# Decoder block with a routed expert stage: the first pair's work moved in between the last tile's steps, the first list made after twelve tiles

## The chip, the cores and the metric

The kernel runs on one NeuronCore of a Trainium2 chip. The time is the device time of one execution in microseconds (us). Engines in the texts: PE (TensorE, matmuls), DVE (VectorE), ACT (ScalarE), POOL (GpSimd) and SP (SyncE, which only issues transfers here). Each engine takes its instructions strictly in the order in which they are written and waits on semaphores. Transfers are issued by SP, ACT and POOL and run on 16 DMA engines that all three share.

## The reference: what is computed

x is 16 tiles of 128 tokens by 256 numbers. A layer norm and a latent self attention are added to x, then a layer norm and a cross attention with 32 heads, then a layer norm and a mixture of 32 experts:

```python
x = x + _L0_attn_ref(_layernorm(x), ...)
x = x + _L0_xattn_ref(_layernorm(x), ctx_2048, ctx_2048, mask, ...)
x = x + _L0_ffn_ref(_layernorm(x), ...)
# in the last: softmax of x @ gate.T, the top experts until their share reaches 0.8 (at most 8),
# for each of them  h = silu(x @ w_gate.T) * (x @ w_up.T);  out += (h @ w_down.T) * weight
```

Tokens pick their own experts, so which rows an expert handles is known only once tokens are routed. The kernel keeps seven experts of each token, so it has 16 x 128 x 7 = 14336 rows to send through experts.

## The kernel before, in words

**Two stages.** In the tile stage 16 tiles pass through both attentions and the router, two or three at a time in flight. In the pair stage 144 blocks of 128 rows, each of one expert, are handled two at a time: 72 pairs, called pair 0 to 71.

**What sets the order.** The tile stage is written by the table `AT`: for each engine it gives every step a time within a tile, and tile b has it `PERIOD` (18.74) times b later. `ORDER` sorts all of them, and each engine's instructions are emitted in that order. The numbers are only a sort key. Steps in `ONCE` stand once. The pair stage is a plain loop over q on each engine, after the table's steps.

**From tile to rows.** For each tile DVE builds `rowb` (the normalized rows, made in `n3`, and the experts' weights, last written in `g13`), and POOL sends it out seven times by index (`sc0` to `sc6`, line 418) to `rows` in memory, into the regions of seven experts. From tile 13 on POOL clears a small buffer between two of them (`pause`, line 416). After tile 15's seven, POOL's queue goes on with the pairs' results (line 428).

**Lists.** Which block belongs to which expert is worked out from the counts in `stack` and `seen4`. A first list of 52 blocks (`NA`) is made by the steps `la1`, `la2`, `la3` on PE and DVE, from the blocks that the first `SEEN` tiles have filled. SEEN is 14 before. A second list of 92 blocks is made within pairs 2 and 4. The blocks are taken in the order of four groups of tiles (`EPOCH`, by the last tile of each), so that tokens of early tiles are finished early.

**One pair q.** SP loads its two blocks to a slot of four (`xblk`, line 313). PE transposes them (`T_`, line 1261), ACT copies that (`xt`), PE multiplies by the expert's gate and up weights (`gu`, line 1283, four matmuls for a block of the two), ACT takes the tanh (`tanh`, line 570), DVE reads the block's weight and target rows (`meta`, lines 920 to 931) and forms the product (`ab`, lines 936 and 942), PE transposes it (`hT_`), ACT copies (`hts`), PE multiplies by the down weights (`dn`, line 1309), ACT copies (`yc`), POOL scatters two blocks of results to `parts` in memory (line 428). A slot of results and of target rows is used again four pairs later: `meta(q)` ends with a write of `dst[q % 4]` (line 931) that waits until both scatters of pair q-4 have landed.

**Final sums.** `FETCH` says in which pair ACT issues the load of a finished tile's seven partial results (896 KB). Three pairs later DVE does `first_sums` (lines 948 and 950), and four pairs later `other_sums` (957, 959, 961), at the end of its iteration. Tiles 12 to 15 are summed after the last pair. SP stores them.

**PSUM.** Five banks form a ring that the tile stage's steps take in PE's order. A step waits until the use five before it has been read.

## Time and profile before

| | us |
|---|---|
| runs shown (3) | 663.89, 668.93, 669.28 |
| median | 668.93 |
| profiled execution, time | 669.07 |
| profiled execution, span | 667.3 |

| engine | busy us | share of the span |
|---|---|---|
| PE | 564.1 | 85% |
| DVE | 421.5 | 63% |
| POOL | 347.5 | 52% |
| ACT | 345.7 | 52% |

The profiled execution lies 0.14 us above the median, and its own time is 1.77 us longer than its span. The busy share is an average over two stages with other limits: PE is nearly always busy in the tile stage (to about 350 us), less so between the stages, and in the pair stage (from 361 us) it has gaps. A row of the timeline gives the start, the length, the engine, the line and the operation, and in brackets how long the engine had been idle before it and what ended that. Busy time is not a reason in itself: each step of the prediction asks which wait ends last.

### The profile page before, as it was taken

Reading aid. Unit: us, or ns where it says so; the run is one execution under the profiler, and the core shown is the slowest. Engines: PE = TensorE matmul, PEld = TensorE weight load, DVE = VectorE, ACT = ScalarE, POOL = GpSimd, SP = SyncE. Lnnn points to the kernel's source line nnn. Section 1 sums busy time; section 2 is a strip of 40 time slices with the busy share of each in tenths; the row PEclk is TensorE's granted clock in tenths of the full one; section 3 lists DMA queues with packets and bytes.
Section 4 is the critical chain, followed back from the end, with each engine's and each line's share of the span. In section 5 each row is a group of like instructions: output and inputs, shape, how many; then the busy total and the mean of one; then the engine's idle time right before and its main releaser. Section 6 shows DMA issues by size and latency. Waiting matters only on the chain.

```text
span 667.3 us, 13791 instructions
## 1 busy us (share of the span) xinstructions
PE 564.1 (85%) x3365; PEld 432.5 (65%) x3365; DVE 421.5 (63%) x1934; ACT 345.7 (52%) x853; POOL 347.5 (52%) x508
## 2 busy tenths in 40 slices
PE   3699999999999999999775869889988888788860
PEld 1467777767777767776554657767767777677750
DVE  1366777778877777877666435444544456774884
ACT  2366667766666767666541425445444454443530
POOL 3122165556656556565556755554544556554551
PEclk9999999999999999999985979999998899997995
DMA  6401337622221212211114757656534468886855
GB/s 177 163 22 44 119 115 209 165 76 64 76 73 64 73 64 78 67 67 66 67 48 139 224 165 233 200 186 184 158 99 130 134 189 280 277 258 209 254 176 182
DMA packets 50750, 93.00 MB, mean 139 GB/s; under 512 B 9991, under 2 KB 39343, under 8 KB 50483
## 3 DMA queue, kind: packets, MB, share of 16 engines
q1 hardware_dynamic: 34642, 43.74, 23.1%
q0 software_dynamic: 12288, 32.15, 13.3%
q10 hardware_dynamic: 3744, 16.24, 7.5%
q8 instruction: 32, 0.52, 0.3%
q14 instruction: 44, 0.35, 0.2%
HBM read 52.73 MB, written 43.54 MB: 144 GB/s over the span
## 4 chain that ended last, share of the span: by engine, by line
PE 61%; issue 10%; ACT 8%; DVE 6%; SPq 5%; DMA 4%; another core or an unknown queue 4%; POOL 1%; POOLq 0%; ACTq 0%; DVEq 0%
PE bank L1283 11%; PE bank L1309 6%; PE bank L1112 5%; ACT KA L514 4%; PE bank L1136 4%; PE bank L1001 4%; PE bank L1113 4%; PE bank L1143 3%; PE bank L1261 3%; PE bank L1162 3%; PE bank L1081 3%; PE bank L1158 3%; ACT Q L436 2%; PE bank L1299 2%
## 5 line engine op out<-in xcount | busy, mean ns | idle before, releaser
L428 POOL DMA_INDIRECT parts<-PT,dst x108 | 109.2, 1011 | 91.9 <-ACT PT L436 57.3
L418 POOL DMA_INDIRECT rows<-rowb,idx x112 | 111.2, 993 | 58.3 <-DVE rowb L814 31.1
L1283 PE MATMUL bank<-wgu_sb,PT 128*128 x576 | 131.3, 353 | 10.2 <-issue 8.8
L1283 PEld LDWEIGHTS bank<-wgu_sb,PT 128*128 128x128 f32 x576 | 95.1, 199 | 28.4 <-issue 27.5
L436 ACT ACTIVATE PT<-bank 128x512 f32<-128x512 f32 (+1 forms) x158 | 77.5, 514 | 51.2 <-PE bank L1309 20.8
L1309 PE MATMUL bank<-wd_sb,VC 96*128 x288 | 79.1, 398 | 21.6 <-ACT VC L436 13.2
L936 DVE SCALAR_TENSOR_TENSOR PT<-PT,bank 128x192 f32<-128x192 f32 x72 | 25.5, 354 | 111.6 <-ACT PT L570 76.9
L714 DVE TENSOR_REDUCE NM<-bank 128x4 f32<-128x512 f32 x128 | 80.5, 681 | 3.0 <-PE bank L1113 2.7
L436 ACT ACTIVATE VC<-bank 96x256 f32<-96x256 f32 (+1 forms) x104 | 46.5, 447 | 63.7 <-PE bank L1299 23.3
L1309 PEld LDWEIGHTS bank<-wd_sb,VC 96*128 96x128 f32 x288 | 52.3, 195 | 32.6 <-issue 27.8
L530 ACT ACTIVATE PT<-bank,padcol 128x512 f32<-128x512 f32 x96 | 59.7, 693 | 15.0 <-PE bank L1143 15.0
L1112 PE MATMUL bank<-KA,Q 96*128 96x512 f32 x128 | 58.6, 458 | 2.8 <-ACT Q L436 0.7
L428 POOL DMA_INDIRECT parts<-wq_sb,dst x36 | 36.6, 1018 | 35.1 <-ACT wq_sb L436 25.1
L1113 PE MATMUL bank<-maskn,nident 128*128 128x512 f32 x128 | 50.7, 396 | 0.0
L1261 PE MATMUL bank<-con,pool_a 128*128 128x128 f32 x288 | 46.5, 287 | 2.7 <-DMA pool_a<-rows 2.0
L570 ACT ACTIVATE PT<-bank 128x192 f32<-128x192 f32 x72 | 23.8, 331 | 47.8 <-PE bank L1283 27.3
L1261 PEld LDWEIGHTS bank<-con,pool_a 128*128 128x128 f32 x288 | 37.5, 148 | 12.7 <-DMA pool_a<-rows 5.7
L942 DVE SCALAR_TENSOR_TENSOR PT<-PT,wsl,bank 128x96 f32<-128x96 f32 x144 | 38.8, 312 | 2.6
L366 POOL TENSOR_TENSOR scalars<-scalars 128x1 f32<-128x1 f32 x64 | 36.9, 576 | 5.0
L364 POOL TENSOR_TENSOR scalars<-mv_ln,scalars 128x1 f32<-128x1 f32 x48 | 9.7, 203 | 57.1 <-DVE mv_ln L620 56.7
L514 ACT ACTIVATE KA<-bank,con 96x128 fp32r<-96x128 f32 x128 | 34.4, 367 | 9.5 <-PE bank L1100 9.5
L436 ACT ACTIVATE Q<-bank 96x512 fp32r<-96x512 f32 (+1 forms) x48 | 34.9, 728 | 6.5 <-PE bank L1121 3.7
(243 smaller groups left out, 1140.4 us busy)
## 6 DMA issues: line engine op xcount, KB each, us to landing
pool_a<-rows SPq DMA_DIRECT2D x144, 148.5 KB
wgu_sb<-wgu_d SPq DMA_DIRECT2D x8, 768.0 KB
pool_a<-parts ACTq DMA_DIRECT2D x5, 896.0 KB
KA<-parts ACTq DMA_DIRECT2D x5, 896.0 KB
...
```

The costliest lines, as they stand in the source:

```text
L418: gp.indirect_dma_start(out=rows, out_offset=bass.IndirectOffsetOnAxis(ap=idx[b % 2][:, k:k + 1], axis=0), in_=rowb[b % 2][:, :], in_offse ...
L428: gp.indirect_dma_start(out=parts, out_offset=bass.IndirectOffsetOnAxis(ap=dst[q % FEED][:, j:j + 1], axis=0), in_=yb[q % FEED][:, j, :], ...
L436: return ac.activation(o, i, ACT.Copy)
L514: last = ac.activation(KA[b % 2][0:CR, g, :], o[0:CR, hf * P:(hf + 1) * P], ACT.Copy, scale=own8[0:CR, g:g + 1])
L530: ac.activation(PT[:, i, :, :].rearrange("p h n -> p (h n)"), ring_bank(f"s{i}", b)[:, :], ACT.Exp, bias=padcol[:, pad_of:pad_of + 1], sca ...
L714: v.tensor_reduce(NM[:, hg, at:at + HG * HG].rearrange("p (g h) -> p g h", h=HG)[:, :, hg], ring_bank(f"mx{u}", b)[:, :].rearrange("p (g m ...
L942: last = v.scalar_tensor_tensor(hv[q % 2][:, j, :], av[q % 2][:, j, :], wsl[q % 2][:, j:j + 1], halves[:, j, NI:2 * NI], ALU.mult, ALU.mult)
L1112: t.matmul(o[:, :], Q2[b % 2][0:CR, hf, hg, :], KA[b % 2][0:CR, HG * hf:HG * hf + HG, :].rearrange("p g m -> p (g m)"), start=True, stop=F ...
L1113: t.matmul(o[:, :].rearrange("p (g m) -> p g m", g=HG), nident[:, :], maskn[:, b * P:(b + 1) * P].unsqueeze(1).to_broadcast([P, HG, P]), s ...
L1261: last = t.transpose(XT_PS[q % 2][:, j * D + k * P:j * D + (k + 1) * P], xblk[q % FEED][:, j, k * P:(k + 1) * P], ident)
L1283: last = t.matmul(GU_PS[q % 2][:, j * 2 * NI:(j + 1) * 2 * NI], xTb[q % 2][:, j, k * P:(k + 1) * P], wgu_sb[:, k, one_of(expert[i]), :].sq ...
L1309: last = t.matmul(Y_PS[q % 2][:, j * D:(j + 1) * D], hTb[q % 2][:, j, :], wd_sb[:, one_of(expert[2 * q + j]), :].squeeze(1), start=True, s ...
```

## The change

Five edits:

1. `EPOCH` becomes (5, 11, 13, 15) and `SEEN` becomes 12. So `la1`, `la2` and `la3`, whose keys hang on SEEN, come two tiles earlier in PE's and DVE's order, and SP's first loads wait for twelve tiles' rows.
2. Steps `T0`, `T1`, `gu0` (PE), `xt0`, `xt1`, `tanh0` (ACT), `meta0`, `ab0` (DVE) enter the table, at places within tile 15. They are the same instructions that stood behind the table's steps.
3. SP waits for the last use of `x1` only before pair 2. The four slots are handed out in another order, so that pairs 0 and 1 don't lie over `x1`.
4. The matmul that places the padding rows (line 1319 before) and the DVE copy of its result come after pair 0's `dn` and after `ab(1)`.
5. `FETCH` puts tiles 6 to 13 at pairs 60, 61, 62, 65, 66, 67, 70, 71. Before it was 57, 59, 61, 63, 65, 67, 69, 71. In DVE's loop `other_sums` now stands ahead of `first_sums`.

```diff
-EPOCH = (5, 10, 13, 15)
-SEEN = EPOCH[2] + 1
+EPOCH = (5, 11, 13, 15)
+SEEN = EPOCH[1] + 1
...
-FETCH = {**{44 + 2 * b: b for b in range(6)}, **{57 + 2 * b: 6 + b for b in range(5)}, **{67 + 2 * b: 11 + b for b in range(3)}}
+FETCH = {**{44 + 2 * b: b for b in range(6)}, **{q: 6 + n for n, q in enumerate((60, 61, 62, 65, 66, 67, 70, 71))}}
...
+           ... "T0": 45.5 + (NB - 1) * PERIOD, "T1": 46 + (NB - 1) * PERIOD, "gu0": 52 + (NB - 1) * PERIOD ...
+           ... "xt0": 47 + (NB - 1) * PERIOD, "xt1": 49 + (NB - 1) * PERIOD, "tanh0": 53 + (NB - 1) * PERIOD ...
+           ... "meta0": 53 + (NB - 1) * PERIOD, "ab0": 57.4 + (NB - 1) * PERIOD ...
...
-        xblk = [... for n in range(FEED)]
+        xblk = [... for n in (2, 3, 0, 1)]
...
-            sp.wait_ge(S["x1b"], NB)
             sp.wait_ge(S["x1nT"], NB)
             for q in range(NPAIR):
+                if q == 2:
+                    sp.wait_ge(S["x1b"], NB)
...
-            xt(0)
-            xt(1)
-            tanh(0)
...
-            meta(0)
-            dve.wait_ge(S["tab"], 5)
-            v.tensor_copy(tbl_i[:, 2 * NBLK:], HT_PS[1][:, 0:NE]).then_inc(S["lists"], 1)
-            ab(0)
             for q in range(NPAIR):
                 if q + 1 < NPAIR:
                     meta(q + 1)
                 late_read(q)
                 if q + 1 < NPAIR:
                     ab(q + 1)
+                if q == 0:
+                    dve.wait_ge(S["tab"], 5)
+                    v.tensor_copy(tbl_i[:, 2 * NBLK:], HT_PS[1][:, 0:NE]).then_inc(S["lists"], 1)
                 late_list(q)
-                if q - 3 in FETCH:
-                    first_sums(FETCH[q - 3])
                 if q - 4 in FETCH:
                     other_sums(FETCH[q - 4])
                     summed.append(FETCH[q - 4])
+                if q - 3 in FETCH:
+                    first_sums(FETCH[q - 3])
...
+            def gu0(_):
+                pe.wait_ge(S["lists"], 1)
+                pe.wait_ge(S["wgu"], 8 * 16)
+                gu(0, 0)
+                gu(0, 1)
...
-            T_(0)
-            T_(1)
-            gu(0, 0)
-            gu(0, 1)
-            vacated(4)
-            pe.wait_ge(S["pick"], 3)
-            t.matmul(HT_PS[1][:, 0:NE], ones[:, :], pickp[:, :], start=True, stop=True).then_inc(S["tab"], 1)
             for q in range(NPAIR):
...
                 dn(q)
+                if q == 0:
+                    vacated(4)
+                    pe.wait_ge(S["pick"], 3)
+                    t.matmul(HT_PS[1][:, 0:NE], ones[:, :], pickp[:, :], start=True, stop=True).then_inc(S["tab"], 1)
```

The first place is PE's queue at the end of tile 15, from its second transpose of the values (`vt1`) to its product `wo`. Before:

```order
L1172 MATMUL bank3<-con,VC 128x128 x3
L996 MATMUL bank4<-con,pool_a 128x128 [waits s_on,s_eall]
L996 MATMUL bank4<-con,pool_a 128x128
L1226 MATMUL bank5<-pick,ones 128x104 [waits s_pick,s_cums]
L1001 MATMUL bank6<-wo_sb,pool_a 128x256 [waits s_oT2_sb,s_on]
L1001 MATMUL bank6<-wo_sb,pool_a 128x256
L996 MATMUL bank7<-con,rowb_1 128x128 [waits s_x2n,s_pt]
```

Now:

```order
L1169 MATMUL bank4<-con,VC 128x128 x3
L1231 MATMUL bank0<-con,pool_a 128x128 [waits s_bl0]
L1231 MATMUL bank0<-con,pool_a 128x128 x3
L1231 MATMUL bank1<-con,pool_a 128x128 [waits s_bl1]
L1231 MATMUL bank1<-con,pool_a 128x128 x3
L993 MATMUL bank5<-con,pool_a 128x128 [waits s_on,s_xT_sb]
L993 MATMUL bank5<-con,pool_a 128x128
L998 MATMUL bank6<-wo_sb,pool_a 128x256 [waits s_oT2_sb,s_eall]
L998 MATMUL bank6<-wo_sb,pool_a 128x256
L1243 TENSOR_LOAD tbl_i [waits s_wgu,s_lists]
L1253 MATMUL bank2<-wgu_sb,PT 128x192
L993 MATMUL bank7<-con,rowb_1 128x128 [waits s_x2n,s_on]
```

The list's matmul (line 1226) has gone from between `oT` and `wo`, eight transposes of pairs 0 and 1 stand ahead of `oT`, and pair 0's gate and up products (the register load and four such matmuls in all, the first shown) stand between `wo` and `xT`.

The second place is DVE's queue in tile 14's stage, between the last normalization of tile 13's heads (`on`) and the eight maxima of tile 14 (line 714 before, 712 now). Before:

```order
L725 TENSOR_TENSOR pool_a<-bank6,rdx_1 128x128 [waits s_rdx]
L675 TENSOR_REDUCE scalars<-bank1 128x1 [waits s_ss]
L714 TENSOR_REDUCE NM<-bank7 128x4 [waits s_cT,s_mx]
L714 TENSOR_REDUCE NM<-bank3 128x4 [waits s_mx]
L714 TENSOR_REDUCE NM<-bank4 128x4 [waits s_mx]
L714 TENSOR_REDUCE NM<-bank5 128x4 [waits s_mx]
```

Now:

```order
L723 TENSOR_TENSOR pool_a<-bank3,rdx_1 128x128 [waits s_rdx]
L854 COPY scalars<-bank4 128x1 [waits s_tab]
L856 TENSOR_TENSOR scalars<-scalars 128x1 [waits s_cums]
L857 SCALAR_TENSOR_TENSOR scalars<-scalars,cob 128x1
L826 TENSOR_SCALAR ge<-cob,scalars 128x52
L860 SCALAR_TENSOR_TENSOR oh,scalars<-cob,scalars,ge 128x52 [waits s_cums]
L829 TENSOR_SCALAR pick<-oh,cob 128x52 [waits s_cums]
L830 SCALAR_TENSOR_TENSOR pick<-cob,scalars,oh 128x52
L673 TENSOR_REDUCE scalars<-bank1 128x1 [waits s_ss]
L712 TENSOR_REDUCE NM<-bank4 128x4 [waits s_cT,s_mx]
```

The seven instructions of `la2` now stand ahead of tile 14's maxima. The four of `la3` come after the fourth of the eight.

The third place is DVE's queue in the pair stage where tiles 6 and 7 are summed, with the pair's own instructions between them left out here. Before, one half of a tile's sums stood in each iteration:

```order
L957 TENSOR_TENSOR VC<-NM 128x256 [waits s_fsum,s_out2]
L959 TENSOR_TENSOR VC<-VC,pool_a 128x256 [waits s_fsum]
L961 TENSOR_TENSOR VC<-VC,x2 128x256 [waits s_fsum]
L948 TENSOR_TENSOR NM<-KA 128x512 [waits s_fin1]
L950 TENSOR_TENSOR NM<-NM,KA 128x512 [waits s_fsum]
```

Those five are now one iteration's (line numbers two lower), with nothing of a pair between them:

```order
L955 TENSOR_TENSOR VC<-NM 128x256 [waits s_fsum,s_out2]
L957 TENSOR_TENSOR VC<-VC,pool_a 128x256 [waits s_fsum]
L959 TENSOR_TENSOR VC<-VC,x2 128x256 [waits s_fsum]
L946 TENSOR_TENSOR NM<-KA 128x512 [waits s_fin1]
L948 TENSOR_TENSOR NM<-NM,KA 128x512 [waits s_fsum]
```

In the iterations of pairs 64, 65, 69 and 70 DVE has both halves to do, and none in those of 60, 61, 62 and 67.

## Rows read from the trace of the kernel before

**Rows 1.** Windows view, core 0: busy time of each engine, PE's granted clock, DMA share
```profile
348.00:350.00 2.00, 0.75 (x7) 0.55 (x7) 1.83 (x12) 0.00 (x0) 1.50 (x3) 1.00 0.12 41
362.00:364.00 2.00, 2.00 (x9) 1.68 (x8) 1.83 (x14) 1.19 (x2) 1.72 (x3) 0.50 0.76 241
388.00:392.00 4.00, 4.00 (x20) 3.65 (x20) 2.57 (x17) 1.18 (x3) 2.75 (x3) 0.72 0.65 183
...
608.90:647.00 38.10, 33.00 (x183) 26.63 (x182) 31.77 (x152) 18.63 (x42) 21.44 (x21) 1.00 0.71 227
```

**Rows 2.** Timeline, pair stage's start: start us, length us, engine, line, operation, idle before
```profile
361.16 1.94 PE L1261 MATMUL bank<-con,pool_a 128*128 128x128 f32 x8
363.02 2.92 PE L1283 MATMUL bank<-wgu_sb,PT 128*128 x8
363.26 0.15 DVE L876 TENSOR_SCALAR cc<-bank 128x2 f32<-128x2 f32 x1
366.64 0.82 PE L1283 MATMUL bank<-wgu_sb,PT 128*128 x4
```

**Rows 3.** Timeline, POOL's chain up to pair 4
```profile
357.89 1.03 POOL L418 DMA_INDIRECT rows<-rowb,idx  x1 [2.41 <-DVE rowb L814]
...
380.27 1.01 POOL L428 DMA_INDIRECT parts<-PT,dst  x1 [0.30 <-issue]
382.64 1.00 POOL L428 DMA_INDIRECT parts<-PT,dst  x1 [1.36 <-ACT wq_sb L436]
...
385.55 0.16 DVE L931 TENSOR_TENSOR dst<-ksl,pool_a 128x2 int32<-128x2 f32 x1 [5.26 <-DMA parts<-PT,dst]
...
386.61 0.80 PE L1246 MATMUL bank<-pick,ones 128*128 128x184 f32 x2 [3.85 <-issue]
```

**Rows 4.** Timeline, tile 15's last steps
```profile
350.21 0.41 PE L996 MATMUL bank<-con,pool_a 128*128 128x128 f32 x2 [1.37 <-DVE pool_a L725]
350.65 0.38 ACT L436 ACTIVATE pool_a<-bank 128x256 f32<-128x256 f32 x1 [3.40 <-PE bank L996]
352.04 1.31 PE L1001 MATMUL bank<-wo_sb,pool_a 128*128 128x256 f32 x4
356.07 0.66 PE L996 MATMUL bank<-con,rowb 128*128 128x128 f32 x2 [2.73 <-DVE rowb L623]
```

**Rows 5.** Timeline of DVE, the list's steps la2 and la3 in tile 15's stage
```profile
349.97 0.15 DVE L856 COPY scalars<-bank 128x1 f32<-128x1 f32 x1
351.35 0.27 DVE L832 SCALAR_TENSOR_TENSOR pick<-cob,scalars,oh 128x52 f32<-128x52 f32 x1
352.24 0.21 DVE L835 CAST tbl_i<-bank 128x52 int32<-128x52 f32 x1 [0.62 <-PE bank L1226]
352.61 0.26 DVE L838 TENSOR_SCALAR mine<-bank,cob 128x52 f32<-128x52 f32 x1
```

**Rows 6.** Timeline of DVE and PE, tile 14's eight maxima and what follows
```profile
311.65 5.01 DVE L714 TENSOR_REDUCE NM<-bank 128x4 f32<-128x512 f32 x8 [0.70 <-PE bank L1113]
316.81 0.63 PE L1121 MATMUL bank<-con,NM 128*128 128x128 f32 x4
```

**Rows 7.** Chain of waits from 596 us: start us, length us, what
```profile
618.52 0.60 DVE NM L948
...
619.76 0.43 DVE con L920 x4
...
620.52 0.16 DVE dst L931
...
621.56 0.35 DVE VC L957
...
622.73 0.04 DVE con L920
...
627.20 5.73 DMA parts<-PT,dst
...
651.79 2.63 DMA parts<-wq_sb,dst
```

More of the change, by code:

```diff
@@ L61 @@
     "SP": {"ldx": -6.0, "ldc": -2.0, "n3": 42.5, **{f"w{n}": 25.0 + 12.0 * n for n in range(10)}}}
-ONCE = {"mi", "mk", "la1", "la2", "la3"} | {f"w{n}" for n in range(10)}
+ONCE = {"mi", "mk", "la1", "la2", "la3", "T0", "T1", "gu0", "xt0", "xt1", "tanh0", "meta0", "ab0"} | {f"w{n}" for n in range(10)}
 ORDER = {e: [(s, b) for _, s, b in sorted((at + PERIOD * b, s, b) for s, at in steps.items() for b in range(NB) if s not in ONCE or b == 0)] for e, steps in AT.items()}
@@ L554, in g1 @@
                 ac.activation(ev[b % 2][:, 0:NE], ring_bank("lg", b)[:, 0:NE], ACT.Exp, bias=nlmax[b % 2][:, :]).then_inc(S["eall"], 1)
-            schedule("ACT", {"mk": mk, "r3": r3, "r7": r7, "r8": r8, "r10": r10, "r11": r11, "r12": r12, "r15": r15, "r16": r16, "r17": q_rows(0), "r17b": q_rows(1),
-                      "kv": kv, "kT": kT, "c": c, **{f"s{i}": s_(i) for i in range(6)}, "pv0": pv(0), "pv1": pv(1),
-                      "oT": oT_, "xT": xT, "g1": g1})
             def xt(q):
@@ L868, in la3, with meta @@
                 listed(0, NA, ring_bank("la3", 0))
-            schedule("DVE", {"la1": la1, "la2": la2, "la3": la3, "mi": mi, "mk": mk, "r1": r1, "r2": r2, "r4": r4, "r5": r5, "r6": r6, "r7": r7, "r9": r9, "r10": r10, "r13": r13, "r14": r14, "r16": r16,
+            def meta(q):
+                dve.wait_ge(S["bl"][q % FEED], 32 * (q // FEED + 1))
+                if 2 * q == NA:
+                    dve.wait_ge(S["lists"], 5)
+                if q >= 2:
+                    dve.wait_ge(S["bv"], nth("bv", q - 2))
+                for j in range(2):
+                    i = 2 * q + j
+                    last = v.scalar_tensor_tensor(wjnk[:, 2 * (q % 2) + j, :], iota_e, tbl_f[:, i:i + 1], xblk[q % FEED][:, j, D:D + NE], ALU.is_equal, ALU.mult,
+                                                  accum_out=wsl[q % 2][:, j:j + 1])
+                last.then_inc(S["w"], 1)
+                for j in range(2):
+                    i = 2 * q + j
+                    last = v.scalar_tensor_tensor(kjnk[:, 2 * (q % 2) + j, :], xblk[q % FEED][:, j, D + NE:D + NE + TOP], mine[:, i:i + 1], iota_k, ALU.is_equal, ALU.mult,
+                                                  accum_out=ksl[q % 2][:, j:j + 1])
+                last.then_inc(S["k"], 1)
+                dve.wait_ge(S["k"], nth("k", q))
+                if q >= FEED:
+                    stored(dve, q - FEED)
+                v.tensor_tensor(dst[q % FEED][:, :], ksl[q % 2][:, :], xblk[q % FEED][:, :, ROW - 1], ALU.add).then_inc(S["dst"], 1)
@@ new lines, in ab @@
+            def ab(q):
+                halves = GU_PS[q % 2][:, 0:4 * NI].rearrange("p (j n) -> p j n", j=2)
+                dve.wait_ge(S["th"], nth("th", q))
+                v.scalar_tensor_tensor(av[q % 2], th[q % 2], 1.0, halves[:, :, 0:NI], ALU.add, ALU.mult).then_inc(S["av"], 1)
+                dve.wait_ge(S["av"], nth("av", q))
+                dve.wait_ge(S["w"], nth("w", q))
+                if q >= 2:
+                    dve.wait_ge(S["hT"], nth("hT", q - 2))
+                for j in range(2):
+                    last = v.scalar_tensor_tensor(hv[q % 2][:, j, :], av[q % 2][:, j, :], wsl[q % 2][:, j:j + 1], halves[:, j, NI:2 * NI], ALU.mult, ALU.mult)
+                last.then_inc(S["bv"], 1)
@@ L871, in _ @@
+            schedule("DVE", {"meta0": lambda _: meta(0), "ab0": lambda _: ab(0), "la1": la1, "la2": la2, "la3": la3, "mi": mi, "mk": mk, "r1": r1, "r2": r2, "r4": r4, "r5": r5, "r6": r6, "r7": r7, "r9": r9, "r10": r10, "r13": r13, "r14": r14, "r16": r16,
                       "kv": kv, **{f"mx{u}": mx(u) for u in range(8)}, "vt0": on(0), "vt1": on(1), "wo": wo_, "n3": n3,
@@ L1285, in gu, with vacated, late @@
                 last.then_inc(S["gu"], 1)
+            def gu0(_):
[3 more added lines that the diff above has]
+                gu(0, 1)
+            schedule("PE", {"T0": lambda _: T_(0), "T1": lambda _: T_(1), "gu0": gu0, "la1": la1, "la2": la2, "la3": la3, "r3": r3, "r4": r4, "r6": r6, "r7": r7, "r8": r8, "r9": r9, "r11": r11, "r12": r12, "r13": r13, "r15": r15, "r16": r16,
+                      "r17": q_half(0), "r17b": q_half(1), "kv": kv, "kT": kT, **{f"mx{u}": mx(u) for u in range(8)}, "c": c,
+                      **{f"s{i}": s_(i) for i in range(6)}, "pv0": pv(0), "pv1": pv(1), "vt0": vt(0), "vt1": vt(1), "oT": oT_, "wo": wo_,
+                      "xT": xT, "lg": lg, "rk": rk_})
+            def vacated(n):
+                last = max(k for k in range(len(USES)) if k % NRING == n)
+                step, of = USES[last]
+                name, k = READ[step]
+                pe.wait_ge(S[name], nth(name, of, k))
+            def late(q):
+                o = HT_PS[q % 2]
+                if q == LATE[0]:
+                    pe.wait_ge(S["grp"], 13)
+                    t.matmul(o[:, 2 * P:2 * P + 1], strict, nmine[:, :], start=True, stop=True).then_inc(S["tab"], 1)
+                elif q == LATE[1]:
+                    pe.wait_ge(S["pick"], 5)
+                    t.matmul(o[:, 2 * P:2 * P + NPICK], ones[:, :], pick[:, :], start=True, stop=True).then_inc(S["tab"], 1)
+            vacated(0)
+            pe.wait_ge(S["snap"], 4)
+            counts(GU_PS[1]).then_inc(S["tab"], 1)
+            pe.wait_ge(S["wd"], 2 * 16)
             def hT_(q):
```

67 lines of the change are left out of this document (9 added, 58 removed), and 2 rows, old and new, of the table AT.

## The prediction, as it was put on record

> **What bounds the kernel now.** I read the windows view first, then the timeline from tile 15's end to pair 5, then the chain of waits of the last 70 us. In the windows [rows 1] PE is the busy engine, 33.0 of 38.1 us in the last eleven pairs at full clock, with DVE close behind at 31.8. So in the pair stage both count. Just ahead of it, at 348 to 350 us, PE is busy 0.75 of 2 us at full clock, and at 362 to 364 us it is busy throughout at a granted clock of 0.50, the lower of its two levels (1.2 GHz), after the gaps that tile 15's last steps leave.
>
> The start of the pair stage looks like PE's: transposes of pairs 0 and 1 for 1.94 us, pair 0's gate and up for 2.92 us, pair 1's at 366.64 [rows 2]. But 20 us later PE stands still for 3.85 us, until 386.61 [rows 3]. What ends that is one chain. POOL begins tile 14's seven scatters at 357.89, when DVE has made `rowb` of tile 14, and sends fourteen of them (tiles 14 and 15) one after another, 22.38 us to the first scatter of results at 380.27, which is 1.60 us each, with no wait. The second scatter of pair 0 goes out at 382.64 (1.36 us idle before it). DVE's write of `dst` for pair 4 needs both landed and comes at 385.55, 5.26 us late, and pair 4's `ab` and `hT` stand behind it. So this is the wait that ends last, and it hangs on the time at which `rowb` of tile 14 is done, not on when pair 0 starts.
>
> **The change, part by part.** The sum is made against the profiled execution's 669.07, 0.14 above the median of the runs.
>
> *Pair 0 between tile 15's steps.* Behind the table's last step PE loses 1.94 + 2.92 = 4.86 us of work [rows 2]. Pair 1's gate and up still waits for DVE's read of the counts in its bank (at 363.26, for 0.15 us [rows 2]), so it starts at about 363.6 where it was 366.64: a lead of 3.0 us for pairs 0 to 3. What that gives the time is nothing: PE reaches pair 4's `hT` 3.0 us earlier and waits 3.85 + 3.0 = 6.9 us for the same `dst`. Bounds: 0 if POOL's chain stays, and −3.0 if it is not what holds PE.
>
> *Where the moved work goes.* `T0` and `T1` fall in the 1.37 us gap ahead of `oT` [rows 4]. Eight transposes took 1.94 us at half clock, so about 1.0 at the full clock that rows 1 shows there: hidden, 0.6 over at half clock. ACT's two copies lie in its 3.40 us of idle [rows 4]. `gu0` falls in the 2.73 us ahead of `xT`: 2.92 us at half clock, so it about fits. If its cover goes, `xT`, the logits and the router of tile 15 come up to 0.4 late, which POOL's queue doesn't feel since tile 14's seven come first. `meta0` is the exception: on DVE it stands between tile 15's last statistics and `n3`, and `rowb` of tile 14 is finished behind `n3`. It takes 620.68 − 619.76 = 0.92 us [rows 7]. `n3` waits for a step of POOL meanwhile, which covers a part that I have no row for: bounds 0 and +0.9, and I take +0.4, near the middle.
>
> *The list's steps out of tile 15.* `wo` could have started when ACT's copy was done, at 350.65 + 0.38 = 351.03 plus 0.15 or so. It started at 352.04, behind the list's matmul, which had waited for DVE's `pick` until 351.62 [rows 4, 5]. That gives back 0.85. With `meta0` this side is −0.45.
>
> *The list's steps into tile 14's stage.* `la2` takes DVE from 349.97 to 351.62, 1.65 us, and `la3` from 352.24 to 352.87, 0.63 us [rows 5]. They now stand ahead of and among the eight maxima, where DVE has only 0.70 us of idle, and the maxima end at 316.66, just as PE starts `c` at 316.81 [rows 6]. So `c` comes 1.65 + 0.63 − 0.70 = 1.6 us late, and with it everything behind, tile 15 and POOL's start too. Bounds: 0 (some later stall takes it up) and +1.6. I take +1.3, near the upper one, since `c` follows the maxima with next to no slack. Together the anchor of POOL's chain moves by +1.3 − 0.45 = +0.85.
>
> *SP.* The first loads waited for tile 13's scatters. Four of them (pairs 0 and 1) now go out in tile 15's stage, once the last `x1nT` is made, the next four after `x1b`. SP's queue has nothing else to do there. POOL's scatters and the padding stores then share the DMA engines with less, so pair 0's second scatter may not lose its 1.36 us [rows 3]. Bounds −1.4 and 0. I take −0.5.
>
> *A longer wait at pair 4.* After the 3.85 us wait the granted clock was 0.72 over 388 to 392 [rows 1]. There are only two levels, and it is already at the lower one when PE goes on: 0, bounds 0 and +1.0.
>
> *The epochs and sums.* The work is the same. A tile's first sums take 619.76 − 618.52 = 1.24 us of DVE, the others 622.73 − 621.56 = 1.17 [rows 7]. Where DVE did one of them in each iteration of pairs 60 to 71, it now does both in 64, 65, 69 and 70. The time per pair in rows 1 is 38.1 / 11 = 3.46 us, of which DVE is busy 31.77 / 11 = 2.89. With one half more that is about 4.1 us, 0.65 above the pair time. The last of the four comes behind `ab(71)` and only delays sums that wait for transfers anyway. In the three others PE's next `hT` waits for DVE: 3 × 0.65 = 2.0. In 60, 61, 62 and 67 DVE has 1.2 us less to do, and PE, which is busy 3.0 of the 3.46, could gain up to 0.4 each where DVE had held it. I credit 0.9 of 1.6: +1.1. Bounds: 0, and 3 × 1.2 = +3.6 where DVE has no slack at all.
>
> *Loads of partial results in bunches.* Three of 896 KB in three pairs, and the loads of tiles 12 and 13 one pair apart instead of two just before the end. Landings of results took 2.63 us at the end but 5.73 us at 627 us, amid such loads [rows 7]. The difference, 3.1 us, is the upper bound for the end. The lower bound is 0. I take +0.5, for one more transfer half in the way.
>
> The Trainium skill, page "DMA: Bandwidth & Descriptors", section "Queues, rings and completion order", says that each DMA engine goes round between the queue rows that have work, a packet at a time. By that rule a second load behind the first on ACT's own queue takes no larger share from POOL's scatters, and this last term would be 0 and the sum 0.5 lower. The trace bears on it only by the 5.73 against 2.63 us, and doesn't separate one load in flight from two.
>
> *Sum:* 0 + 0.85 − 0.5 + 0 + 1.1 + 0.5 = +1.95, so **671.0 us**.
>
> **The rivals.**
>
> *The forecast (0.50).* Lead swallowed at pair 4, small costs elsewhere: 671.0. With the bounds of the small terms it lies between 667.5 and 674.5.
>
> *The lead survives (0.20).* POOL's scatters of results go out sooner or land sooner, because the loads have left the DMA queues when they run. For it: the 1.36 us of idle between the two scatters of pair 0 has no wait in the code behind it, and DVE's 5.26 us wait is a transfer's. Against it: fourteen scatters at 1.60 us each run back to back on POOL and no part of the change shortens them. Price: −3.0 − 1.4 and the +0.85 anchor, 669.07 − 3.55 = 665.5. If also PE's 3.85 us shrinks (scatters landing at once), down to 661.7.
>
> *Slower: DVE becomes the bound of the last pairs (0.18).* One mechanism: in iterations 64, 65 and 69 DVE has 2.89 + 1.2 = 4.1 us or more, its `ab` comes late, PE waits in `hT`, and results land later, so slots come free later. It decides when DVE's queue has no slack before `ab`, as at 618.5 to 623, where the chain of waits runs through DVE without a gap [rows 7]. Price: +3.6 and the 3.1 of slow landings with +0.85 give 669.07 + 7.5 = 676.6.
>
> *The change doesn't do what it says (0.12).* The first loads, held by POOL's landings or by tile 15's `x1nT`, come so late that `T0` blocks PE ahead of `oT`. Then what is moved is only put in the way: if it is just late enough to cost nothing and win nothing, 669.1 to 670.
>
> **Numbers.** About 1% (6.7 us) is what a measurement of this kernel can tell from no change: under 662.4 is faster, over 675.6 slower. Of the surviving lead a third reaches that, and the runs shown spread over 5.4 us, so another tenth is from sources I don't have a row for: faster 0.16. Slower: most of that rival and a little of the forecast: 0.18. Within 1%: 0.66. The range goes from 661.7, the low end of the second case, to 677, just past the third's price: **661.7 to 677**.
>
> **What would show it.** Right: pair 1's gate and up starts 3 us earlier relative to the last router step, yet PE waits 6 to 7 us ahead of pair 4's `hT`, and DVE's `dst` wait is longer than 5.26. POOL's first scatter of results still comes 22.4 us after its first of tile 14. Tile 14's `c` comes about 1.3 us late, and the gap between `oT` and `wo` of tile 15 shrinks by 0.8. Pairs 64 to 66 and 69 to 70 take over 4 us each. Wrong: if PE's wait at pair 4 is no longer than 3.85 us, my view of POOL's chain falls and the time is near 665. If pairs 60 to 71 take 38 us or less as before, the term of the sums falls.

## The result and the profile after

The changed kernel takes 674.34 us, the median of 20 runs (664.28 to 680.53). The kernel before, run beside it 20 times, takes 665.89 (659.94 to 670.21). The ratio is 1.0074 with a 95% interval of 1.0042 to 1.0106, so about 5 us slower. (Some executions of either kernel are slower as a whole; the ratio compares only the others, and so says less than the 8.5 us between the two medians.) The forecast was 671.0, range 661.7 to 677.0. Measured once more in the second group of experiments, the ratio was 1.0133 (1.0067 to 1.0199). Weighted, the two give 1.0085 ± 0.003, some 5.7 us.

The profiled execution of the changed kernel (680.53 us, span 678.6) lies 6 us above its own median, so the two traces differ by 11.3 us, more than the kernels do. A stretch counts below only where several traces agree on it.

Where the time went up to the pair stage is easiest to see in the timeline of DVE and PE in tile 14's stage (start us, length us, engine, line, operation, idle before it). It answers to [rows 5, 6].

```profile
311.13 0.15 DVE L854 COPY scalars<-bank 128x1 f32<-128x1 f32 x1
313.28 0.28 DVE L673 TENSOR_REDUCE scalars<-bank 128x1 f32<-128x128 f32 x1
313.48 2.48 DVE L712 TENSOR_REDUCE NM<-bank 128x4 f32<-128x512 f32 x4
315.87 0.21 DVE L833 CAST tbl_i<-bank 128x52 int32<-128x52 f32 x1
316.40 2.48 DVE L712 TENSOR_REDUCE NM<-bank 128x4 f32<-128x512 f32 x4
319.03 0.63 PE L1118 MATMUL bank<-con,NM 128*128 128x128 f32 x4 [0.21 <-DVE NM L712]
```

`la2` (from 311.13 to 313.28) and `la3` (from 315.87) push the maxima back, and tile 14's `c` (line 1118) comes 2.2 us later than in [rows 6]. Counted from tile 13's `c` it comes after 21.88 us, where it was 19.94.

About 10 us on, another thing happens, which the forecast did not have. First the timeline of SP and ACT, then the chain of waits at the same place, then the windows (busy time of PE, PEld, DVE, ACT, POOL, then PE's granted clock, DMA share, GB/s).

```profile
325.71 5.24 SPq L314 DMA_DIRECT2D pool_a<-rows  x4
331.77 0.60 ACT L437 ACTIVATE VC<-bank 128x512 f32<-128x512 f32 x1 [4.29 <-remote]
```

```profile
327.21 4.54 another core or an unknown queue
```

```profile
326.00:334.00 8.00, 4.25 (x35) 3.21 (x34) 4.17 (x19) 2.18 (x5) 6.86 (x9) 0.91 0.59 193
334.00:342.00 8.00, 7.97 (x26) 5.89 (x25) 5.53 (x10) 0.98 (x2) 0.35 (x1) 0.66 0.05 20
```

ACT stands still for 4.29 us, and what ended that is put to no engine. The kernel before has the same stall at the same instruction, but shorter:

```profile
328.01 0.60 ACT L436 ACTIVATE VC<-bank 128x512 f32<-128x512 f32 x1 [2.55 <-remote]
```

```profile
326.00:334.00 8.00, 5.24 (x35) 4.40 (x34) 6.13 (x22) 2.17 (x4) 5.25 (x6) 1.00 0.24 97
334.00:342.00 8.00, 6.08 (x29) 4.81 (x29) 5.05 (x19) 3.13 (x5) 1.99 (x4) 0.82 0.00 0
```

What differs most is the traffic: the DMA share is 0.59 against 0.24, since SP's first four loads of rows now go out at 325.71. The granted clock after the stall is 0.66 against 0.82, and PE is busy 7.97 of 8 us to get through its backlog. Tile 15's `c` follows at 342.43, 23.40 us after tile 14's (19.93 before). Not all of that is the longer stall. fetch_only, a kernel below whose tile stage is that of the kernel before, has the stall at 2.56 us and still 22.26 us between these two `c`, with a granted clock of 0.85 between them where the trace of the kernel before has 1.00.

POOL's chain answers to [rows 3] (timeline):

```profile
363.47 1.03 POOL L419 DMA_INDIRECT rows<-rowb,idx  x1 [4.37 <-DVE rowb L812]
385.87 1.01 POOL L429 DMA_INDIRECT parts<-PT,dst  x1 [0.30 <-issue]
388.29 1.00 POOL L429 DMA_INDIRECT parts<-PT,dst  x1 [1.42 <-issue]
390.83 0.16 DVE L887 TENSOR_TENSOR dst<-ksl,pool_a 128x2 int32<-128x2 f32 x1 [7.10 <-DMA parts<-PT,dst]
391.89 0.98 PE L1281 MATMUL bank<-pick,ones 128*128 128x184 f32 x2 [3.66 <-DVE PT L898]
```

The start of tile 14's scatters has moved from 357.89 to 363.47, by 5.6 us. From there the first scatter of results comes 22.40 us later (22.38 before), and the second loses 1.42 us as before. DVE waits 7.10 us for `dst` where it was 5.26. PE's wait is 3.66, about as long as before: its lead of 2.7 us at pair 0 had shrunk to 1.5 by pair 3. A part of it went by the clock, which was granted at 0.50 over 366 to 370 and 0.55 over 370 to 374, up to some 10 us behind the first scatter of tile 14; in the kernel before it was back at 0.96 over 366 to 370, 8 us behind it.

Tile 15's end answers to [rows 4]:

```profile
351.88 1.04 PE L1231 MATMUL bank<-con,pool_a 128*128 128x128 f32 x8
354.20 0.41 PE L993 MATMUL bank<-con,pool_a 128*128 128x128 f32 x2 [1.28 <-DVE pool_a L723]
355.17 1.10 PE L998 MATMUL bank<-wo_sb,pool_a 128*128 128x256 f32 x4 [0.56 <-ACT pool_a L437]
356.56 2.92 PE L1253 MATMUL bank<-wgu_sb,PT 128*128 x8 [0.29 <-issue]
361.30 0.41 DVE L621 TENSOR_SCALAR rowb<-x,mv_ln,scalars 128x256 f32<-128x256 f32 x1 [2.64 <-DMA rows<-rowb,idx]
```

The transposes take 1.04 us and are hidden, `oT` to `wo` is 0.97 where it was 1.83, and `gu0` takes 2.92 us. The last row is new: `n3` no longer waits for POOL's statistics but for tile 13's last scatter, issued at 357.21, to land, before it may overwrite `rowb`. The chain of waits of the changed kernel (start us, length us, what) runs through this landing to POOL's first scatter of tile 14:

```profile
355.59 0.97 POOL rows L419
357.21 3.99 DMA rows<-rowb,idx
363.47 1.03 POOL rows L419
```

The last pairs answer to the last line of [rows 1]:

```profile
612.54:658.16 45.62, 35.93 (x184) 29.33 (x183) 29.72 (x148) 19.12 (x42) 22.75 (x23) 0.93 0.66 215
```

That is 45.62 us for eleven pairs, 7.5 more than before. The chain of waits names a load of rows in it, behind three loads of partial results in a row (`617.74 11.64 DMA pool_a<-rows`), but the same program profiled again took 40.39 us for them:

```profile
615.05:655.44 40.39, 33.44 (x183) 26.46 (x183) 29.67 (x148) 18.72 (x42) 22.84 (x24) 1.00 0.74 246
```

So of the 7.5 some 5 are that one execution's. Of the forecast's sign, over 4 us for pairs 64 to 66 and 69 to 70, one half came: `dn` of pairs 66 and 67 follows 4.31 and 4.22 us after the one before it (3.68 and 3.04 in the kernel before), that of pair 71 after 3.74 (3.65).

### The profile page after: what moved, and what is told of

Its sections match the earlier page's. It is cut to its first block, busy times and chain, and to the rows that moved or that the text cites. A ratio compares the mean times of both kernels' runs of the same rounds, so it can differ in the third digit from the quotient of the medians.

```text
span 678.6 us, 13790 instructions
## 1 busy us (share of the span) xinstructions
PE 569.1 (84%) x3365; PEld 438.0 (65%) x3365; DVE 422.2 (62%) x1934; ACT 345.1 (51%) x853; POOL 346.9 (51%) x508
## 4 chain that ended last, share of the span: by engine, by line
PE 54%; issue 11%; SPq 9%; ACT 8%; DMA 5%; DVE 5%; POOL 5%; another core or an unknown queue 3%; POOLq 0%; ACTq 0%; DVEq 0%
PE bank L1253 8%; PE bank L1109 5%; PE bank L1310 4%; ACT KA L515 4%; PE bank L1110 4%; PE bank L1133 4%; PE bank L998 4%; PE bank L1140 3%; SPq L313 3%; POOL rows L419 3%; PE bank L1078 3%; PE bank L1159 2%; PE bank L1231 2%; PE bank L1155 2%
## 5 line engine op out<-in xcount | busy, mean ns | idle before, releaser
L1253 PE MATMUL bank<-wgu_sb,PT 128*128 x576 | 135.4, 361 | 10.0 <-issue 8.3
L1253 PEld LDWEIGHTS bank<-wgu_sb,PT 128*128 128x128 f32 x576 | 99.2, 206 | 26.4 <-issue 25.5
L437 ACT ACTIVATE PT<-bank 128x512 f32<-128x512 f32 (+1 forms) x158 | 77.9, 514 | 62.7 <-PE bank L1310 26.8
L1109 PE MATMUL bank<-KA,Q 96*128 96x512 f32 x128 | 60.1, 469 | 2.4 <-DVE scalars L854 0.6
```

The source lines that it names most:

```text
L437: return ac.activation(o, i, ACT.Copy)
L1109: t.matmul(o[:, :], Q2[b % 2][0:CR, hf, hg, :], KA[b % 2][0:CR, HG * hf:HG * hf + HG, :].rearrange("p g m -> p (g m)"), start=True, stop=F ...
L1253: last = t.matmul(GU_PS[q % 2][:, j * 2 * NI:(j + 1) * 2 * NI], xTb[q % 2][:, j, k * P:(k + 1) * P], wgu_sb[:, k, one_of(expert[i]), :].sq ...
```

## The experiments

All stretches below are differences of starts in each run's own trace: `c` is line 1118 of the changed kernel or its counterpart, "A" is from tile 13's `c` to POOL's first scatter of tile 14, "B" from there to DVE's `dst` of pair 4, "M" from there to `dn` of pair 60, "E" from there to `dn` of pair 71. All in us. "Clock there" is the clock granted to PE between the `c` of tiles 14 and 15, as a share of full.

| kernel | c 13 to 14 | c 14 to 15 | clock there | A | B | M | E | ratio to before (95%) |
|---|---|---|---|---|---|---|---|---|
| before | 19.94 | 19.93 | 1.00 | 61.0 | 27.7 | 223.3 | 38.1 | 1 |
| fetch_only | 19.88 | 22.26 | 0.85 | 62.7 | 27.6 | 219.9 | 41.0 | 1.0060 (1.0022, 1.0097) |
| double_sums | 19.92 | 22.17 | 0.85 | 62.6 | 27.3 | 216.1 | 40.4 | 1.0052 (1.0020, 1.0085) |
| bunch_loads | 19.94 | 21.23 | 0.92 | 61.3 | 27.3 | 222.7 | 39.0 | 1.0013 (0.9979, 1.0048) |
| changed | 21.88 | 23.40 | 0.85 | 66.3 | 27.4 | 221.7 | 45.6 | 1.0074 (1.0042, 1.0106) |
| after_again | 21.87 | 23.48 | 0.85 | 67.0 | 27.3 | 224.9 | 40.4 | 1.0133 (1.0067, 1.0199) |
| fetch_back | 21.86 | 22.87 | 0.85 | 65.5 | 27.3 | 230.8 | 39.6 | 1.0108 (1.0067, 1.0150) |
| no_move | 21.87 | 23.17 | 0.85 | 65.4 | 27.9 | 215.6 | 38.7 | 1.0115 (1.0076, 1.0153) |
| no_pause | 21.87 | 22.89 | 0.85 | 65.6 | 33.3 | 222.0 | 38.9 | 1.0159 (1.0115, 1.0203) |
| hold_loads | 21.85 | 22.27 | 0.85 | 65.4 | 27.3 | 225.2 | 40.8 | 1.0101 (1.0045, 1.0157) |
| late_list | 20.09 | 21.87 | 0.92 | 63.5 | 27.6 | 223.2 | 39.6 | 1.0033 (0.9992, 1.0074) |
| hold_late | 20.07 | 22.70 | 0.85 | 63.8 | 27.5 | 222.0 | 40.0 | 1.0058 (1.0020, 1.0095) |
| late_fetch | 20.12 | 20.60 | 1.00 | 61.0 | 27.5 | 225.6 | 38.7 | 1.0081 (1.0052, 1.0110) |
| late_fetch_nomove | 20.07 | 22.85 | 0.85 | 63.3 | 27.7 | 219.9 | 38.2 | 1.0010 (0.9974, 1.0047) |

The clock column explains much of the one beside it. The first four rows have one and the same tile stage, and their `c` of tile 15 comes after 19.93 us with the clock at 1.00, 21.23 at 0.92, 22.17 and 22.26 at 0.85. What made the clock fall in three of these four executions and not in the fourth, all with ACT's stall of 2.55 to 2.58 us there, is open.

The first group came after the first reading of the trace, when the last pairs looked like the cause.

**fetch_only**: the kernel before, with this alone.

```diff
-FETCH = {... **{57 + 2 * b: 6 + b for b in range(5)}, **{67 + 2 * b: 11 + b for b in range(3)}}
+FETCH = {... **{q: 6 + n for n, q in enumerate((60, 61, 62, 65, 66, 67, 70, 71))}}
...
-                if q - 3 in FETCH: first_sums(...)
                 if q - 4 in FETCH: other_sums(...)
+                if q - 3 in FETCH: first_sums(...)
```

> The kernel before with only the new FETCH (tiles 6 to 13 loaded at pairs 60, 61, 62, 65, 66, 67, 70, 71) and the new order of the sums; EPOCH, SEEN and pair 0 as before. Loads theory: three loads of 896 KB in a row hold back SP's loads of rows, PE waits for them around pairs 62 to 64; pairs 60 to 71 take 42 to 46 us instead of 38.1, and the whole is 4 to 7 us slower than before (ratio 1.006 to 1.010). DVE theory (the forecast's): +1.1 to +1.6 us, PE waits behind ab in pairs 64, 65 and 69, and not for rows. Third view: the last pairs were long in the changed kernel only because everything ahead of them had shifted; then 0.

Measured: +4.0 us (1.5 to 6.4), pairs 60 to 71 in 41.0 us. So regrouping the loads and sums costs something by itself; which of the two, this run doesn't say.

**fetch_back**: the changed kernel with the loads spread.

```diff
-enumerate((60, 61, 62, 65, 66, 67, 70, 71))
+enumerate((58, 59, 61, 63, 65, 67, 69, 71))
```

> The changed kernel with the loads spread as before as far as the epochs let them (58, 59, 61, 63, 65, 67, 69, 71). Loads theory and DVE theory alike get back what the bunches cost: by the loads theory 4 to 7 us faster than the changed kernel, so at or just below the kernel before (ratio to before 0.997 to 1.003) with pairs 60 to 71 at 38 to 40 us. If the loss lies in the tile stage and at tile 14's maxima: still +3 to +5 us against before (1.005 to 1.008).

Measured: not faster than the changed kernel (1.0108 against 1.0074 and 1.0133), although the last pairs took 39.6 us. The loads theory, as the main cause, fell here: A was 65.5 us as in the changed kernel, where the four traces with the old list order have 61.0 to 62.7.

**no_move**: the changed kernel with pair 0's steps behind the table (`xt0`, `xt1`, `tanh0`, `meta0` and `ab0` in the same way).

```diff
-"T0": 45.5 + (NB - 1) * PERIOD, "T1": 46 + (NB - 1) * PERIOD, "gu0": 52 + (NB - 1) * PERIOD
+"T0": 90 + (NB - 1) * PERIOD, "T1": 91 + (NB - 1) * PERIOD, "gu0": 92 + (NB - 1) * PERIOD
...
```

> The changed kernel with pair 0's transposes, gate/up, tanh, meta and ab placed behind all steps of the table again; all else as changed. Forecast's theory (POOL's chain of fourteen scatters holds pair 4, the lead is worth nothing): the same as the changed kernel within 1 us, PE's wait at pair 4 about 3 us shorter than there. Rival (the lead is worth something): 2 to 3 us slower than the changed kernel. A second rival: faster by 1 to 3 us, since meta and gate/up of pair 0 no longer stand ahead of tile 15's normalization and transposes, so tile 14's rowb is complete sooner.

Measured: 1.0115, between the two measurements of the changed kernel (1.0074 and 1.0133). PE's wait at pair 4 is 3.18 us, only 0.5 shorter than there and not the 3 expected. B is 27.9 us with pair 0's `dn` 10.5 us after the first scatter of tile 14, and 27.4 in the changed kernel with `dn` 8.3 us after it. The lead is there and is gone at pair 4.

**no_pause**: the changed kernel without cleared buffers between scatters.

```diff
-PAUSE_FROM = 13
+PAUSE_FROM = NTOK // P
```

> The changed kernel without the twelve-plus cleared buffers between POOL's scatters of tiles 13 to 15 (PAUSE_FROM beyond the last tile). They carry no data. If POOL's queue of fourteen scatters is what holds pair 4: it shortens from 22.4 to about 18 us (14 x 1.27), results go out 4 us sooner, DVE's wait for dst of pair 4 shrinks from 7.1 to 3 us and the whole is 3 to 4 us faster than the changed kernel. If what holds pair 4 is the landing of transfers (the DMA engines are full), the scatters only queue there: no gain, or a loss of 1 to 3 us from closer traffic on the row loads.

Measured: 1.0159, slower. POOL's chain did shorten, to 17.91 us, but the timeline of ACT and POOL shows what came instead:

```profile
379.86 1.01 POOL L429 DMA_INDIRECT parts<-PT,dst  x1 [0.30 <-issue]
381.17 1.00 POOL L429 DMA_INDIRECT parts<-PT,dst  x1 [0.30 <-issue]
384.80 0.60 ACT L437 ACTIVATE PT<-bank 128x512 f32<-128x512 f32 x1 [10.75 <-remote]
389.29 0.98 POOL L429 DMA_INDIRECT parts<-PT,dst  x1 [7.12 <-ACT PT L437]
```

ACT stands for 10.75 us, again ended by nothing that the profile names, while scatters run without a pause, and everything behind it waits. One trace shows this. This pointed to the stall at 331.77 in the changed kernel: it is 4.24 to 4.29 us in all of the changed, fetch_back, no_move and no_pause, and 2.55 or 2.56 in the kernel before and fetch_only.

**after_again**: the changed kernel unedited, as the yardstick of the second group.

> The changed kernel itself once more, beside the three others of this group. Expected at a ratio of 1.007 (1.004 to 1.011) to the kernel before, with ACT's stall of 4.2 to 4.3 us ahead of its copy at 330 to 332 us (2.55 in the kernel before), tile 15's c 22.9 to 23.4 us after tile 14's, and pairs 60 to 71 in 39 to 46 us.

Measured: 1.0133, stall 4.23 us, `c` 23.48 us after `c`, and 40.4 us for the last pairs.

**hold_loads**: SP's first loads wait for tile 15's `c`.

```diff
             sp.wait_ge(S["x1nT"], NB)
+            sp.wait_ge(S["Q3c"], nth("Q3c", NB - 1))
```

> The changed kernel with one wait more on SP: its first loads of rows (four of 148.5 KB) go out only when ACT has copied tile 15's c, about 12 us later, still ahead of pair 0's transposes. Theory (the four loads at 325.7 us share the DMA engines with the load of ACT's next instructions, which lengthens ACT's stall there from 2.55 to 4.26 us, and PE, left without work, goes on at half clock): the stall goes back to 2.5 to 2.6, tile 15's c comes 20 to 21 us after tile 14's instead of 23.4, POOL starts tile 14's scatters 2.5 to 3.5 us earlier, and the time falls by 2.5 to 3.5 us, to a ratio of 1.002 to 1.004. Rival (the stall belongs to where the instructions lie, not to traffic): it stays at 4.26 and nothing is gained. Second rival (gain given back, since the loads now run beside tile 13's scatters, whose landing tile 15's normalization waits for): stall gone, time unchanged.

Timeline of ACT and SP:

```profile
328.37 0.60 ACT L438 ACTIVATE VC<-bank 128x512 f32<-128x512 f32 x1 [1.46 <-PE bank L1160]
330.53 0.59 ACT L438 ACTIVATE Q<-bank 96x512 fp32r<-96x512 f32 x1 [1.57 <-remote]
343.50 15.34 SPq L315 DMA_DIRECT2D pool_a<-rows  x10
```

With the loads away the copy to `VC` comes 9.9 us after tile 14's `c` instead of 12.7, a stall of 1.57 us follows one copy later, and tile 15's `c` is 22.27 us behind instead of 23.48. So the loads lengthen that stall in this kernel. Holding them gives back 1.2 us there, not the 2.5 to 3.5 expected, and 1.5 us in A against after_again, but nothing against no_move and fetch_back, which load early and have 65.4 and 65.5 too. The time (1.0101 against 1.0133) can't tell that from nothing.

**late_list**: `la2` and `la3` behind tile 14's maxima.

```diff
     "PE": {...
-           "la2": 80 + (SEEN - 1) * PERIOD, "la3": 86.2 + (SEEN - 1) * PERIOD},
+           "la2": 90.2 + (SEEN - 1) * PERIOD, "la3": 94.3 + (SEEN - 1) * PERIOD},
     "DVE": {...
-           "la2": 83 + (SEEN - 1) * PERIOD, "la3": 86.5 + (SEEN - 1) * PERIOD},
+           "la2": 93 + (SEEN - 1) * PERIOD, "la3": 97 + (SEEN - 1) * PERIOD},
```

> The changed kernel with la2 and la3 put behind tile 14's maxima in DVE's and PE's order (7 to 12 us later), where DVE has idle time. Forecast's theory of their cost: tile 14's c comes 19.9 to 20.2 us after tile 13's again instead of 21.9, so 1.9 us are got back there. Since the list is ready later, SP's first loads also go out later than the load of ACT's instructions: if those collided, ACT's stall falls to 2.6 to 3.4 as well and the gain is 3 to 5 us in all (ratio 1.000 to 1.004); if not, 1.9 us (1.004 to 1.006). Rival (what DVE loses there is taken up by later stalls): no gain in the time although c is earlier.

Timeline of DVE, PE and ACT:

```profile
311.62 5.02 DVE L712 TENSOR_REDUCE NM<-bank 128x4 f32<-128x512 f32 x8 [0.67 <-PE bank L1110]
316.79 0.63 PE L1118 MATMUL bank<-con,NM 128*128 128x128 f32 x4
319.61 0.15 DVE L854 COPY scalars<-bank 128x1 f32<-128x1 f32 x1
329.19 0.59 ACT L437 ACTIVATE Q<-bank 96x512 fp32r<-96x512 f32 x1 [2.30 <-remote]
```

Measured: `c` is back at 20.09 us, the stall at 2.30, A at 63.5. The ratio is 1.0033 against 1.0133 beside it and 1.0085 over both measurements: 3.5 us less, give or take 3.4. That is the 3 to 5 us expected, and the largest part of the loss that one edit gives back. The loads went out at 326.94 in this run, so it was not by their absence that the stall shrank; why it did is open. Two more pairs of runs differ in the place of the list's steps alone, hold_loads and hold_late, fetch_back and late_fetch. Both go the same way (1.0101 to 1.0058, 1.0108 to 1.0081), and the three together give 2.7 us, give or take 2.1.

**hold_late**: both edits together.

```diff
+            sp.wait_ge(S["Q3c"], nth("Q3c", NB - 1))
...
+           "la2": 90.2 + ..., "la3": 94.3 + ...
```

> Both of the above: la2 and la3 behind the maxima, and the first loads held until tile 15's c is copied. If the two costs are separate and carry through: POOL's first scatter of tile 14 comes at 358 to 359 us as before the change (363.5 in the changed kernel), ratio 0.998 to 1.002. If the anchor comes back but the time stays above 1.004, the loss lies in the pair stage (bunched loads and sums). If the lead of pair 0 then shows too: 0.994 to 0.998.

Measured: 1.0058, A 63.8. Holding the loads adds nothing once the list is late. The first loads go out at 342.47, and yet ACT has its stall, 2.41 us long, where late_list with its loads at 326.94 has 2.30. In this pair traffic makes no difference to it.

**late_fetch**: late_list with the spread loads of fetch_back.

```diff
+           "la2": 90.2 + ..., "la3": 94.3 + ...
...
+enumerate((58, 59, 61, 63, 65, 67, 69, 71))
```

> The changed kernel with la2 and la3 behind tile 14's maxima and with the loads of partial results spread again (58, 59, 61, 63, 65, 67, 69, 71). Theory (most of the loss was the list's steps and what they set off in tile 15; the bunches cost 1.6 to 2 us more): ratio 0.997 to 1.002, pairs 60 to 71 in 38 to 40 us. If the bunches cost nothing: as late_list, 1.003. If pair 0's lead were worth its 3 us in the pair stage: 0.993 to 0.996.

Measured: 1.0081, although A is 61.0 and E 38.7, both as before the change. Its time went into M, 225.6 us. None of the three expectations fits.

**late_fetch_nomove**: that, with pair 0's steps behind the table.

```diff
+"T0": 90 + (NB - 1) * PERIOD, "T1": 91 + (NB - 1) * PERIOD, "gu0": 92 + (NB - 1) * PERIOD
```

> The same with pair 0's steps behind the table again. Forecast's theory (lead swallowed at pair 4 by POOL's chain of scatters): DVE's dst of pair 4 comes 27.3 to 27.9 us after POOL's first scatter of tile 14 here too, though pair 0 starts 2 to 2.6 us later against it; time as late_fetch within 1.5 us. Rival (the move is worth something): 2 to 3 us slower than late_fetch.

Measured: 1.0010, about 4.7 us faster than late_fetch (the intervals of the two don't meet), with B at 27.7. So on this base the move seems to cost. On the changed kernel's base (no_move) the difference is 2 us the other way, give or take 3. Both pairs together give a cost of 1.5 us, give or take 2.2, which can't be told from nothing.

**double_sums**: the kernel before, both halves of a tile's sums in one iteration.

```diff
-                if q - 3 in FETCH:
+                if q - 4 in FETCH:
                     first_sums(FETCH[q - 4])
-                if q - 4 in FETCH:
                     other_sums(FETCH[q - 4])
```

> The kernel before with the loads where they were, and both halves of a tile's sums in one iteration, four pairs after the load: DVE has 2.4 us more in every second iteration and none between. By the forecast's term (0.65 us for each doubled iteration whose PE waits behind ab, less 0.4 where there are no sums): six such iterations in pairs 61 to 71 give +1.5 to +4 us, pairs 60 to 71 in 40 to 42 us, ratio 1.002 to 1.006. Rival (the doubling is free, the transfers cost): 0, pairs 60 to 71 at 38 to 39 us.

Timeline of DVE and PE in such an iteration:

```profile
625.53 0.54 DVE L942 SCALAR_TENSOR_TENSOR PT<-PT,wsl,bank 128x96 f32<-128x96 f32 x2
626.12 0.42 PE L1298 MATMUL bank<-con,PT 128*96 128x128 f32 x2 [0.65 <-DVE PT L942]
```

Measured: +3.5 us (1.3 to 5.7), pairs 60 to 71 in 40.4 us. PE waits for `ab`, here 0.65 us. The expectation counted six doubled iterations. The edit doubles twelve, six in pairs 48 to 58 and six in 61 to 71, and the 3.5 us belong to all of them.

**bunch_loads**: the kernel before, with the loads of tiles 6, 7 and 8 at pairs 57, 58, 59 and its sums unmoved.

```diff
+SUMS = {... as FETCH was}
+FETCH = {**SUMS, 58: 7, 59: 8}
+FETCH.pop(61)
```

> The kernel before with the sums where they were, and the loads of tiles 6, 7, 8 at pairs 57, 58, 59 instead of 57, 59, 61: three loads of 896 KB in three pairs. Loads theory: SP's loads of rows and POOL's scatters are slowed, PE waits for rows around pairs 59 to 62, +1 to +3 us. DVE theory: 0. Some of the cost may be given back, since pair 61 then has no load.

Measured: 1.0013, no difference; from `dn` of pair 56 to that of 62 it took 24.5 us against 25.7. The doubled sums cost, the bunched loads of three don't by anything that shows; the interval leaves room for up to 3 us.

## Why the forecast held, point by point

*The lead is swallowed at pair 4 (0).* Right in its mechanism. B is 27.3 to 27.9 us in all thirteen traces with the pauses, whether pair 0's `dn` came 8.3 or 11.9 us after tile 14's first scatter. "PE waits 6 to 7 us" was wrong: 3.66, since part of the lead went on the way, by the low clock among others. By the forecast's own sign (a wait no longer than 3.85 us) its view of POOL's chain would have fallen. The sign was badly chosen, since PE can lose its lead anywhere ahead of pair 4; DVE's wait for `dst` (7.10 against 5.26) and B bear the chain out. M is 215.6 to 223.3 us in the six traces where pair 0's steps follow the table (mean 219.6) and 221.7 to 230.8 in the eight where they stand in it (mean 224.4). The two groups differ in ACT too: the stalls put to the unnamed queue between 400 and 610 us sum to some 12 us in the mean of the six and 19 in that of the eight, and PE's idle that ACT ended to 5 and 11. But a trace is one execution. Those of the six lie 1.6 us below the medians of their own runs in the mean (no_move's, with the shortest M, 6.3 below), those of the eight 3.3 above. That is 4.9 us of difference where M has 4.8. So the pattern in M is no more than how far each trace lies from its own median, and doesn't show that the move costs. Only late_fetch and late_fetch_nomove, whose traces lie within 1.2 us of their medians, are left with 5.7 us in M and 4.7 in the times; that was not measured again, and no_move says otherwise.

*meta0 (+0.4) and `la3` out of tile 15 (−0.85).* The gap from `oT` to `wo` shrank by 0.86, as forecast. It gave nothing, because another wait now ends last, which the forecast had not seen. These are the rows of DVE's sum that `n3` needs, in the changed kernel and in the kernel before:

```profile
356.31 0.42 DVE L730 TENSOR_TENSOR x<-bank,x 128x256 f32<-128x256 f32 x1 [2.26 <-issue]
```

```profile
353.38 0.42 DVE L732 TENSOR_TENSOR x<-bank,x 128x256 f32<-128x256 f32 x1 [0.52 <-PE bank L1001]
```

Counted from tile 15's `c` it comes 2.8 us earlier than before (13.9 against 16.6), and still `n3` starts no earlier (18.9 against 18.8), since it waits for tile 13's last scatter. That scatter goes out 14.75 to 14.91 us after tile 15's `c` in all thirteen traces with the pauses. In the nine of them that have the new list, DVE then stands idle for 1.41 to 3.17 us until it has landed, and `n3` starts 3.3 to 4.6 us after its issue. `meta0` lies inside that idle time and costs nothing, and POOL's chain begins there with tile 13's scatters and not with tile 14's. From tile 15's `c` to POOL's first scatter of tile 14 it takes 20.6 us in the mean of the four traces with the old list (20.1 to 21.2), 20.4 in the two without the move, and 21.05 in the eight with it (20.3 to 21.6). So this side is about +0.5 where I had −0.45, and what sets it is how long a scatter takes to land. The loads of pairs 2 and 3, which edit 3 lets go at 354.10, run beside it (DMA share 0.58 over 354 to 358, 0.20 before); whether they lengthen it no run shows.

*`la2` and `la3` into tile 14 (+1.3).* This is the step that failed, by size. At `c` of tile 14 it is 1.95 us, the same to 0.03 in six traces, where I had worked out 1.6: `la2` holds the next instruction up for 2.15 us there (311.13 to 313.28) and `la3` for 0.53 (315.87 to 316.40), and 2.15 + 0.53 − 0.70 is 1.98. And it does not end there. A is 61.0 to 62.7 (mean 61.9) without it, 65.4 to 67.0 (mean 65.9) with it, and 61.0 to 63.8 (mean 62.9) in the four where the steps come later. So the anchor moved by 4.0 us and not by 0.85: 1.95 at tile 14's `c`, 1.6 from there to tile 15's (23.0 in the mean of six against 21.4 of four), and 0.4 behind it. Putting the two steps behind the maxima gives 3.0 of A back.

*SP and the DMA engines (−0.5).* Wrong in sign. I had written that SP's queue has nothing else to do there, and looked only at whose loads leave the later stage, not at what they meet in the earlier one. They meet ACT's stall: 2.55 to 2.58 us in the four traces without them, 4.23 to 4.29 in the five with them and the list in its new place. With the list late it is 2.3 us with them in two traces, missing in a third, and 2.4 without, so the loads alone don't make it long. And the stall is not all of the 1.6 us: at a clock of 0.85 tile 15's `c` comes after 22.2 us with the old list and after 22.9 to 23.5 in these five, some 1 us more; the rest is that two of the four old traces had more of the clock. The second scatter of pair 0 lost its 1.42 us all the same, so nothing was relieved.

The profile counts two queues for instructions (q8 and q14), and I take the stall for ACT waiting on its next instructions; no row ties it to one of their packets, and in the kernel before no packet of either queue is listed from 324 to 330 us, so that is argued, not shown. The Trainium skill, page "Runtime: NRT & Kernel Launch", section "Instruction fetch mechanics", says that each engine's sequencer fetches its next block over a DMA queue of its own, at a cost "mostly hidden". If the stalls of 1.57 to 10.75 us are such fetches, they fit the first half and not the second; no run here shows that they are.

*Sums doubled (+1.1) and loads bunched (+0.5).* E is 38.1 to 39.6 us in the five traces with single sums (mean 38.7; three of them have one doubled iteration, at pair 62, and one has the bunched loads), and 38.7 to 45.6 (median 40.2) in the eight with the new order: about +1.5 us, the 1.6 that I had for both. double_sums puts it at the sums: 3.5 us for twelve doubled iterations is 0.3 each, and its E, 40.4, is 1.7 to 2.3 us longer for the six in it, 0.3 to 0.4 each, where I had 0.65. The rule that the prediction cites from the Trainium skill (page "DMA: Bandwidth & Descriptors", section "Queues, rings and completion order") would make a second load on ACT's queue cost nothing. bunch_loads agrees as far as it can: 1.0013 (0.9979 to 1.0048), which doesn't tell the 0.5 us of the term from nothing.

*The sum.* With 4.0 in place of 0.35 for anchor and SP, it would have been 5.6 us, where about 5 (first measurement) and 5.7 (both, weighted) were measured. The forecast had the direction but a third of the size, 1.95. That its 671.0 lies only 3.3 us from the median of 674.34 is partly luck: it was added to 669.07, which is 3.2 us above the 665.89 that the kernel before took beside it. The range was wide: it would have held any time from 7 us faster to 8 us slower than that base. The bounds that the forecast gives for its small terms add up to 666.8 to 678.4, not to 667.5 to 674.5. The rival of DVE as the bound had the right place for a part of the loss and the wrong price: 1.5 us, not the 6.7 of its two terms. The surviving lead fell with B. So the forecast's case was the right one of the four, and a slower anchor, for which I had given a bound of 1.6, was most of the loss.

None of the versions beats the kernel before. The best of those with the new list, late_fetch_nomove, can't be told from it.
